# A graph-attention layer with sorted nodes: more buffers for the ranks, work between VectorE, ScalarE and TensorE dealt anew

## The reference

```
XW = X @ W;  s_col = XW @ a[0, :f];  s_row = XW @ a[0, f:]          # X, H: 2048 x 128
den = exp(leaky_relu(s_row[:, None] + s_col[None, :], 0.01))         # 2048 x 2048
num = A @ den                                                        # A: 2048 x 2048
att = where(num != 0, den / num, 0)
out = layernorm(X + A @ (att @ XW))
```

## Time and profile before

| what | us |
|---|---|
| median of 3 runs | 309.93 (309.92 to 310.09) |
| the profiled execution's own time | 310.36 |
| its span in the profile | 308.6 |
| TensorE matmul, busy | 273.2 |
| VectorE, busy | 224.5 |
| ScalarE, busy | 190.1 |
| GpSimd, busy | 96.0 |

### The profile page before, as it was taken

One profiled execution on the slowest core, in us unless ns is written; L12 is line 12 of the kernel. 1 busy time (PEld: TensorE's weight loads), 2 busy tenths in 40 slices (PEclk: granted clock), 3 DMA queues, 4 the chain that ended last, 5 costly groups with the idle time before them and its releaser, 6 DMA issues.

```text
span 308.6 us, 5025 instructions
## 1 busy us (share of the span) xinstructions
PE 273.2 (89%) x1635; PEld 155.1 (50%) x1635; DVE 224.5 (73%) x363; ACT 190.1 (62%) x245; POOL 96.0 (31%) x95
## 2 busy tenths in 40 slices
PE   8793589788699999999999999999999726999994
PEld 3592337233244544544454445444444202999994
DVE  0778899999789989987985789898797710052275
ACT  2498068698899986959586788879688630000001
POOL 6501277998884644500000000066000063000000
PEclk9855556999999999999999999999999986999998
DMA  5000599707665343510000000001000053201111
GB/s 169 1 2 2 146 322 387 303 3 219 181 201 156 93 139 88 158 63 0 0 2 0 0 2 0 0 29 43 0 2 1 0 170 106 66 2 36 34 36 34
DMA packets 13940, 24.65 MB, mean 80 GB/s; under 512 B 1760, under 2 KB 8288, under 8 KB 13920
## 3 DMA queue, kind: packets, MB, share of 16 engines
q0 software_dynamic: 5632, 18.88, 19.1%
q1 hardware_dynamic: 8288, 5.50, 6.1%
HBM read 21.23 MB, written 3.15 MB: 79 GB/s over the span
## 4 chain that ended last, share of the span: by engine, by line
PE 62%; DVE 7%; ACT 6%; POOL 5%; issue 4%; DMA 4%; ACTq 1%; POOLq 0%; SPq 0%
PE ps L486 25%; PE ps L510 9%; PE ps L546 9%; PE ps L548 5%; PE ps L504 4%; POOL A L314 3%; PE ps L480 2%; PE ps L448 2%; PE ps L446 2%; PE ps L490 2%; DMA A<-adjT,perm 2%; POOL d_b L335 2%; ACT A L607 1%; ACT tmp L626 1%; DMA D<-d_b 1%
## 5 line engine op out<-in xcount | busy, mean ns | idle before, releaser
L486 PE MATMUL ps<-A,D 128*128 x372 | 86.3, 379 | 0.9 <-issue 0.2
L486 PEld LDWEIGHTS ps<-A,D 128*128 x372 | 36.2, 97 | 40.9 <-issue 10.1
L314 POOL DMA_INDIRECT A<-adjT,perm x31 | 45.5, 1468 | 28.3 <-DVE A L206 12.6
L335 POOL DMA_INDIRECT d_b<-crow,ranku x16 | 17.6, 1099 | 109.1 <-DVE crow L1014 71.0
L685 ACT ACTIVATE stage<-ps 128x1024 f32<-128x1024 f32 (+1 forms) x33 | 32.9, 997 | 25.8 <-PE ps L490 25.7
L996 DVE SCALAR_TENSOR_TENSOR stage<-ps,stage 128x1024 f32<-128x1024 f32 (+1 forms) x33 | 39.2, 1188 | 12.8 <-ACT stage L697 12.7
L546 PE MATMUL ps<-D,A 128*128 128x256 f16 x256 | 42.4, 273 | 1.0 <-DMA D<-d_b 1.0
L548 PE MATMUL ps<-D,A 128*128 128x128 f16 x256 | 42.3, 219 | 0.0
L1000 DVE SCALAR_TENSOR_TENSOR stage<-rrow,cfloor,stage 128x1024 f32<-128x1024 f32 (+1 forms) x33 | 41.3, 1252 | 1.3
L206 DVE SCALAR_TENSOR_TENSOR A<-A,ecol 128x1024 f16<-128x1024 f32 x31 | 38.8, 1277 | 1.0 <-ACT A L607 0.4
L687 ACT ACTIVATE stage<-stage,epst 128x1024 f32<-128x1024 f32 (+1 forms) x33 | 37.1, 1123 | 1.1
(11 more groups left out here) (187 smaller groups left out, 367.9 us busy)
## 6 DMA issues: line engine op xcount, KB each, us to landing
tmp<-xT SPq DMA_DIRECT2D x4, 256.0 KB, 4.1
d_xw<-stage SPq DMA_DIRECT2D x1, 1024.0 KB, 5.1
D<-d_b SPq DMA_DIRECT2D x4, 256.0 KB, 3.7
out<-crow SPq DMA_DIRECT2D x3, 256.0 KB, 2.3
A<-adjT,perm POOLq DMA_INDIRECT x31, 5.6
xws<-d_xw,perm POOLq DMA_INDIRECT x16, 3.6
d_b<-crow,ranku POOLq DMA_INDIRECT x16, 2.5
out<-crow SPq DMA_DIRECT2D x1, 128.0 KB, 1.8
```

What stands on the lines that cost most here:

```text
L314: nc.gpsimd.indirect_dma_start(out=raw[n], out_offset=None, in_=rows, in_offset=bass.IndirectOffsetOnAxis(ap=perm[:, 0, h, b:b + 1], axis= ...
L486: nc.tensor.matmul(num[bank + c], D[:, d, bass.ds(slot, 1), :], A[:, h, bass.ds(k, 1), a, c * W:(c + 1) * W], start=False, stop=False, ski ...
```

## The change

- `RING = 5` flag buffers, two of them in A's second half. ScalarE sums blocks 0 to 9 (`OWN = 10`).
- Of the 16 one-hots of r, VectorE makes 9 (`AHOT = 9`), and ScalarE makes 7 with a Square (L612 of the new file) and a Relu (L615) each.
- The counts behind the stairs are made by TensorE: `tot`, then `upto`, `p_lohi`, `p_slots`, each with a small copy or compare between. VectorE's broadcast compares and reductions (L867, L868, L886, L889, L891) go, and two instructions of `scales`.
- `den_logs(0)`, `den_logs(1)` and `weights(0)` read c's row in PSUM. The copy to `crow` stands behind `weights(0)`. ScalarE loads 20 numbers of `jk` first and 11 in tile 0 of the main loop.
- `OWN_CASTS = 1`: ScalarE casts n = 14 too.
- Tile 0 opens its banks with a product with zeros, and its products of weights and sums come last.

```diff
-OWN_CASTS = 2
+OWN_CASTS = 1
-OWN = 11
+RING = 5
+OWN = 10
+AHOT = 9
+        flags = ([D[...][:, i * N:(i + 1) * N].bitcast(BF16) for i in range(3)]
+                 + [A[:, 1, b, :, :].rearrange("p a i -> p (a i)").bitcast(BF16) for b in (NB - 2, NB - 1)])
 # TensorE, place_sorted
+                    if i == 0 and b >= AHOT:
+                        pe.wait_ge(S["hots_act"], b - AHOT + 1)
+                        pe.wait_ge(S["hots"], AHOT)
 # TensorE, behind p_pre
-            keep_warm(10, 2)
+            for j in range(NB):
+                mm = nc.tensor.matmul(num[3][0:NB, 0:1], hot3[:, :, j], onesb[:, :], start=(j == 0), stop=(j == NB - 1))
+            mm.then_inc(S["tot"], 1)
+            keep_warm(4, 2)
+            pe.wait_ge(S["tot_sb"], 1)
+            nc.tensor.matmul(num[1][0:NB, 64:65], tri[0:NB, 0:NB], total, start=True, stop=False)
+            nc.tensor.matmul(num[1][0:NB, 64:65], ident[0:NB, 0:NB], total, start=False, stop=True).then_inc(S["upto"], 1)
+            keep_warm(4, 2)
+            pe.wait_ge(S["cmp_lohi"], 1)
+            pe.wait_ge(S["rst_sb"], 1)
+            nc.tensor.matmul(num[0][:, 0:2 * NB], ones16[0:NB, :], upto_flags, start=True, stop=True)
+            nc.tensor.matmul(num[3][0:NB, 0:1], upto_flags[:, 0:NB], ones16[0:NB, 0:1], start=True, stop=True).then_inc(S["p_lohi"], 1)
             place_sorted(1)
+            pe.wait_ge(S["cmp_slots"], 1)
+            nc.tensor.matmul(num[3][:, 64:64 + NS], ones16[0:NB - 1, :], slot_flags, start=True, stop=True).then_inc(S["p_slots"], 1)
             keep_warm(4, 2)
 # TensorE, main loop
-            pe.wait_ge(S["w_lo"], 1)
             pe.wait_ge(S["d_lo"], 2)
+                    if t == 0:
+                        nc.tensor.matmul(num[bank + c], ident[0:1, 1:1 + P // 2].bitcast(F16), E[0:1, 0:4, :]..., start=True, ...)
+                        continue
+                if t == 0:
+                    pe.wait_ge(S["w_lo"], 1)
+                    pe.wait_ge(S["sums_sb"], 2)
 # ScalarE
+            act.wait_ge(S["low_places"], 1)
+            for b in range(AHOT, NB):
+                nc.scalar.activation(far[:, b - AHOT, :], ramp16[:, 0:P], ACT.Square, bias=place[:, 1, b:b + 1], scale=-1.0).then_inc(S["far"], 1)
+            for b in range(AHOT, NB):
+                act.wait_ge(S["far"], b - AHOT + 1)
+                nc.scalar.activation(lowhot[:, b, :], far[:, b - AHOT, :], ACT.Relu, bias=onesr[:, 0:1], scale=-1.0).then_inc(S["hots_act"], 1)
             act.wait_ge(S["ccol_sb"], 1)
             act.wait_ge(S["flags_sum"], OWN)
             (the two copies of XW, xw_sb)
+            act.wait_ge(S["tot"], 1)
+            nc.scalar.copy(total, num[3][0:NB, 0:1]).then_inc(S["tot_sb"], 1)
-            nc.scalar.copy(crow[:, :], ps[:, 4:8, :].rearrange("p c w -> p (c w)")).then_inc(S["crow_sb"], 1)
-            act.wait_ge(S["crow_sb"], 1)
+            jc = list(columns(0, BATCH[2][1]))
             weights(0)
+            nc.scalar.copy(crow[:, :], crow_ps).then_inc(S["crow_sb"], 1)
+                if t == 0:
+                    jc.extend(columns(BATCH[2][1], NS))
 # VectorE
-                if b >= 3:
-                    dve.wait_ge(S["flags_used"], b - 2)
-                    dve.wait_ge(S["flags_sum"], min(b - 2, OWN))
+                if b >= RING:
+                    dve.wait_ge(S["flags_used"], b - RING + 1)
+                    dve.wait_ge(S["flags_sum"], min(b - RING + 1, OWN))
+            dve.wait_ge(S["upto"], 1)
+            V.tensor_scalar(upto_flags, ..., num[1][0:NB, 64:65], None, ALU.is_ge).then_inc(S["cmp_lohi"], 1)
             mark_places(1, rankc[:, :])
+            dve.wait_ge(S["p_lohi"], 1)
+            V.tensor_scalar(slot_flags, ..., ALU.subtract, ALU.is_gt).then_inc(S["cmp_slots"], 1)
```

More of the change, by code:

```diff
@@ L155, in graph_attention_layernorm @@
         onesr = xws[:, 1792:1792 + P]
-        flags = [D[:, :, :, :].rearrange("p a s j -> p (a s j)")[:, i * N:(i + 1) * N].bitcast(BF16) for i in range(3)]
+        flags = ([D[:, :, :, :].rearrange("p a s j -> p (a s j)")[:, i * N:(i + 1) * N].bitcast(BF16) for i in range(3)]
+                 + [A[:, 1, b, :, :].rearrange("p a i -> p (a i)").bitcast(BF16) for b in (NB - 2, NB - 1)])
         lowhot = flags[0].rearrange("p (b j) -> p b j", b=NB)
+        far = zlate[:, :].bitcast(BF16).rearrange("p (b j) -> p b j", j=P)
         hot = flags[2][:, 0:NB * NB]
@@ L189, in graph_attention_layernorm @@
         names = """b_late warm_sb p_rst rst_sb slot_hot p_slot in_w in_x0 in_x1 in_x2 in_x3 in_ws in_c p_wa wa_sb p_row p_col r_even r_odd rcol_sb ccol_sb p_xw xw_sb xw_out
-            const ramp flags flags_used flags_sum own vals_r vals_c pv where hots p_place perm_r perm_c rs_ready cs_ready thr hot p_pre top p_top rowtop cmax crow_t crow_sb
+            const ramp flags flags_used flags_sum own vals_r vals_c pv where low_places far hots_act tot tot_sb upto cmp_lohi p_lohi cmp_slots p_slots hots p_place perm_r perm_c rs_ready cs_ready thr hot p_pre top p_top rowtop cmax crow_t crow_sb
             slots_ready mask_ready hi_done hi_dve lo_dve e_zero e_hi e_ready p_sums sums_hi sums_sb
@@ L390, in _ @@
             for b in range(NB):
-                fl = flags[b % 3]
+                fl = flags[b % RING]
                 pe.wait_ge(S["flags"], b + 1)
@@ L487, in add_num @@
                                              start=False, stop=False, skip_group_check=True)
+                if t == 0:
+                    pe.wait_ge(S["w_lo"], 1)
+                    pe.wait_ge(S["sums_sb"], 2)
+                    for c in cols:
+                        o = h * H + c * W
+                        nc.tensor.matmul(num[bank + c][:, 0:HW], wgt[0:R, J * P:(J + 1) * P], sums[0:R, o:o + HW],
+                                         start=False, stop=False, skip_group_check=True)
                 for c in cols:
@@ L777, in mark_places @@
                                 vals[:, i, :, :].unsqueeze(3).to_broadcast([P, NB, 5, NB]), ALU.mult)
-                for b in range(NB):
+                for b in range(NB if i else AHOT):
                     V.tensor_scalar(lowhot[:, b, :], ramp16[:, 0:P], place[:, 1, b:b + 1], None, ALU.is_equal
```

66 lines of the change are left out of this document (34 added, 32 removed).

## The result

The changed kernel took 308.71 us (median of 15 runs, 307.90 to 310.31) against 310.32 us (309.74 to 312.22, 15 runs) for the kernel before, run beside it: ratio 0.9956, 95% interval 0.9942 to 0.9971. The ratio makes it 1.4 us faster (the medians 1.6), where 6.6 us slower was forecast. Four repeats in later hours, on three chips, gave 1.0188, 0.998, 1.0136 and 1.0197. Ratios compare fast runs with fast runs: the 0.998 rests on two of six executions (310.11 and 311.18 us), and that repeat's median was 315.82 against 311.38 us. The profiled execution is of the first comparison: 309.03 us, span 307.3 (before 310.36 and 308.6).

A forecast was written before the change was run, and what follows sets the result against it. From 90 us TensorE bounds the kernel, so the column's start decides. Square(0) 6.5 us later plus 0.1 for tile 1 gives +6.6 us, from 310.36 to 316.96, median 316.5; range 310.0 to 318.3.

The forecast's parts named there:

- The hold: POOL's late gathers wait until DVE's long row of residuals ends; ScalarE's cast of n = 14 then delays its list 6.8 us.
- rival A: Gathers meeting the long row of residuals are held until it ends: about 316.5 us, chance 0.75.
- the same in small: Gather n = 14 read as held across two residuals, ending 0.9 us after DVE turned to the copy L902.
- Ranks: DVE's ranks, with five flag buffers, end at 27.98 instead of 29.58: 1.6 us earlier.
- One-hots: Fourteen ScalarE instructions, 4.3 us, ahead of XW's copies: `xw_sb` at 35.4, `perm_r` and the gathers 1.9 us later.
- Counts: Counts going round TensorE and ScalarE cost DVE 0.4 to 0.5 us, and again a gather meeting the long product.
- L902, now L946: DVE's copy ahead of the long row of residuals, waiting for `p_slot`: about 56.1 instead of 55.88.
- Copy of c's row: Behind `weights(0)` on ScalarE it costs 1.8 us in place of a 2.09 us wait: net -0.3.
- Loads in tile 0: Eleven register loads on ScalarE in tile 0, perhaps 1.1 us: +0.1, between 0 and +0.6.
- Tile 0's order: TensorE may start before the sums are split, but Square(0) waits for ScalarE's own list: worth 0.
- Rival B: No hold: gathers get in between residuals, at most 1.3 us late; +0.4 for Square(0), 310.4 us, chance 0.15.
- rival C: ScalarE's one-hots take 0.167 us each, not 0.31, so the permutation comes 2.0 us sooner: 308.4 us, chance 0.10.

The follow-up runs named there:

- b_paced: The kernel before, with gather n of r's side, from n = 10 on, held until residual n - 10: 317.0 us, kernel before 314.26.
- b_pause: The kernel before, with gather 7 waiting for c's permutation: 312.39 us, kernel before 315.52.
- a_noslot: The changed kernel, with the slots counted on VectorE as before, without TensorE's short product: 325.82 us, kernel before 313.54.
- p_crow: The kernel before, with c's row read from PSUM and copied behind `weights(0)`: 311.49 us, kernel before 311.38.
- a_third: The changed kernel unaltered, repeated on a third chip or in a third hour: 315.82 us, kernel before 311.38.
- a_pause: The changed kernel, with gather 7 (and those behind it) waiting for c's permutation: 316.5 us, kernel before 315.52.
- a_pause2: As a_pause, with gather 11 also waiting until VectorE has read the slot values: 315.48 us, kernel before 315.52.
- a_tile0: The changed kernel, with the main loop's first tile in its old order: ratio 1.0105 to the kernel before.
- n_crow: The changed kernel, with c's row copied to SBUF first and the copy read, as before: 319.75 us, kernel before 314.26.
- b_again: The kernel before, unchanged, profiled once more: 316.67 us.
- a_dve16: The changed kernel, with all 16 one-hots of r on VectorE and none on ScalarE: ratio 0.9893 to the kernel before.
- a_again: The changed kernel unaltered, repeated beside the kernel before: 319.55 us, kernel before 314.26.

## Why the prediction was wrong

**The step that failed is "The hold"**, +6.8 us and rival A's 0.75. It took one row, n = 15 with 11.75 us, for what always happens when a gather meets a long row of residuals. The mechanism exists. Four of the 20 profiles have it: before, b_paced, b_pause (9.36 us) and a_noslot, each time ending 0.8 us behind DVE's row. But in the sixteen others, the profile after among them, the gather that met the long row went through 0.9 us behind the next border between two residuals, and those behind it in step. The trace of the kernel before had such a case as well, gather n = 16:

```profile
69.13 1.41 POOL L314 DMA_INDIRECT A<-adjT,perm  x1 [0.31 <-issue]
```

It met two residuals, 68.44 to 70.92, and was through at 70.54, before they ended. The prediction didn't look at it.

The reading of n = 14, "the same in small", was sound for its place. In twelve profiles a gather starts within the first of the two residuals ahead of L902 (now L946), and all twelve were through 0.8 us behind the end of the two. Four of these had started 0.4 to 1.1 us ahead of the border between the two and passed it by (p_crow, a_third, a_pause, a_pause2: 2.53 and 3.16 to 3.17 us). What didn't follow is that a long row does the same. The rule of the Trainium skill ("SBUF — State Buffer", "Who interferes with whom"), by which the two exclude each other for one whole instruction, fits the sixteen, and neither these four nor the four long holds. Which of the two a gather meets is open. Three of the long holds began 1.09 us into a residual, and the sixteen 0.1 to 0.95 us into one. But a_noslot's hold began 0.77 us in, where p_crow's gather, 0.78 us in, went through.

**The other steps, by their order.** *Ranks*: the last flags ended at 28.70, not 27.98. The work began 0.62 us later in this execution, so 0.1 of the step itself is off. *One-hots*: right in mechanism and size, 0.29 us each and not 0.315, and `xw_sb` at 35.98. The sixteen products took 1.25 us and not 1.9, since nothing paced them. The first gather came within 0.13 us of the forecast by luck: 0.75 us less of work from the first compare, and a start 0.62 us later. *Counts*: right, DVE waits 0.49 us for the sum, and the gather that meets the long product takes 2.02 us. *L902, now L946*: 55.43 against 56.1, since c's row took 4.50 us and not 5.24: TensorE's granted clock rose from 0.50 to 1.00 when 1.6 us of it had passed, and not 3.2 as before. *Copy of c's row*: right, it fills the wait. *Loads in tile 0*: they ran beside Exp (83.40 to 84.63) and held Square(1) by 0.2, against +0.1. *Tile 0's order*: put at 0, and worth 0.27 us at Square(1) by a_tile0's trace.

**Rival B's mechanism happened, and its sum was 1.9 us too high.** The lines for the largest term:

```profile
53.38 4.98 ACT L651 ACTIVATE A<-A,ecol 128x1024 f16<-128x1024 f32 x4 [1.08 <-DMA A<-adjT,perm]
58.78 0.31 ACT L686 ACTIVATE cs<-cs,sc 128x16 f32<-128x16 f32 x1 [0.42 <-issue]
```

```profile
57.21 0.02 ACT A L651
57.23 0.04 issue
57.27 1.46 ACTq L661
```

Cast 9 started at 57.21 and ended at 58.36, not at 57.85: 0.5 later. But the register loads (ACTq, 1.46 us) ran beside it. Before, the copy of c's row stood between the two, and the loads waited for it. So the next instruction came 0.4 us behind cast 9, where B had the 1.8 us that were left of copy and loads: 1.4 less. The sixteen relus from PSUM were 0.8 us shorter than before's, to which the prediction gave no term at all; n_crow puts 0.7 of it on the source. And Square(0) had waited some 0.2 us for TensorE's tile 0 before (82.65, behind 82.53), which the prediction read as the same moment; now it doesn't wait. That makes 0.5 - 1.4 - 0.8 - 0.2 = -1.9. A faster result by more than 0.2% had been given 0.08, as rival C alone, and C did not happen (0.29 us per tile).

**What none of the theories had** is that TensorE's increments come late while gathers run. In this first comparison neither profile has it. In later hours it stood in the kernel before too, but at another place and less often: by 8 to 9.5 us in b_again, and by 2.1 and 2.4 in p_crow, where next to nothing waited. Ahead of c's permutation it stood in all eleven later profiles that have seven one-hots on ScalarE and no pause at gather 7 (waits of 2.45 to 11.35 us), in neither with the pause, in none of the five of the order before, and not in a_dve16.

The profile after has the seven one-hots and no stall, so they alone don't make it. A closer mark is in the traces. The ninth gather (n = 8) in a_again, then in the profile after, and there the last products:

```profile
47.95 0.96 POOL L321 DMA_INDIRECT A<-adjT,perm  x1 [0.30 <-issue]
```

```profile
49.45 0.93 POOL L321 DMA_INDIRECT A<-adjT,perm  x1 [0.30 <-issue]
```

```profile
47.96 0.78 PE L422 MATMUL ps<-D 128*128 128x80 bf16 x6 [0.20 <-DVE D L832]
```

In all eleven with the stall gather 8 started 0.6 us before the products for c's permutation ended, in the other nine it started 0.7 us or more behind their end. Counted from the first gather, the products ended after 10.2 us in the order before, after 10.7 in the profile after and in a_dve16 (where gather 5 had met the long product and lost 1.1 us), and after 11.3 in the eleven. The change has DVE wait for TensorE's counts ahead of the placing (0.49 us in the profile after), which works that way. The mark was looked for only when the stalls were known. The two pauses, which also took gather 8 away, fit it, but no run moved gather 8 alone, and why the increment waits is open. DVE's program length and the short product are excluded. The late increments for c's row, the slot values and the sums have no such mark.

## What to carry to other kernels

A long wait seen once is a possibility, not a rule: look in the same trace for the same pair of instructions that did not wait, profile the unchanged kernel again, check that the repeat really meets the case, and give both outcomes a chance. Compare times of two traces from the first piece of work, not from the start of the span. Where a stretch has the DMA engines saturated, price each handover through TensorE there as a risk, and run a repeat on another chip before believing a gain of half a per cent. Read ahead of a stall "who waited and for whom": two engines that start in the same 0.05 us, on different semaphores of a third, point at the third.

## What the runs showed of the hardware

- TensorE's semaphore updates can be recorded up to 11.6 us behind the end of their products (a_noslot) while gathers run. The DMA share was near 1.0 in the long ones ahead of c's permutation, 0.6 to 0.9 in that of a_dve16 (2.0 us). Two gathers fewer issued removed a stall of 10.4 us.
- A gather on GpSimd beside back-to-back VectorE instructions either goes through at a border and then in step with them (0.94 us each, residuals at 1.24 and not 1.20 us) or waits for the end of the whole row and 0.8 us more: 9.36 to 17.47 us in all for long rows, 2.2 to 3.2 us for the first two residuals.
- A relu of 128x128 with a column offset from a register takes 0.25 us from PSUM and 0.29 from SBUF (2.00 and 2.34 per eight, to the start of what follows).
